# Earlier weight checks and a flag moved ahead of one group; in the chosen experts the shared rows added by VectorE and the inverse roots taken for two tiles together

## The chip, the core and the metric

One core of a Trainium2 chip runs the whole program. The metric is the device time of that core in microseconds; lower is better. PE is TensorE's matmul side and PEld its weight loads, DVE is VectorE, ACT is ScalarE, POOL is GpSimd, SP is SyncE, which here issues most DMAs.

## The reference, cut to what matters

Four residual layers over x of 16 x 512 rows of 128 numbers. The first is attention, the second a gated MLP with ternary weights, the third a mixing layer by Fourier transforms, the fourth a mixture of eight experts of which each row takes one, beside a shared expert:

```python
x = x + _layernorm(attention(_layernorm(x), ...))
x = x + _layernorm(ternary_mlp(_layernorm(x), ...))
x = x + _layernorm(fourier_mix(_layernorm(x), ...))
# the fourth layer, on h = _layernorm(x)
shared_out = swiglu(h, shared_gate, shared_up, shared_down)
logits = h @ gate_w.T
top_id = argmax(logits); score = sigmoid(max(logits))
routed_out = swiglu(h * score, r_gate[top_id], r_up[top_id], r_down[top_id])
x = x + _layernorm(shared_out + routed_out)
```

`swiglu(x, wg, wu, wd)` is `silu(x @ wg.T) * (x @ wu.T) @ wd.T`, with 256 hidden numbers. Everything is fp32.

## The kernel before

**Stages.** The program runs through attention (64 groups: 16 chunks of 512 rows, four groups of heads each), the MLP in pairs of chunks, the mixing and the routing, and last the chosen experts. Each engine has a program of its own, written by hand, and the engines meet at semaphores. An engine works strictly in the order written: whatever waits holds back everything behind it on that engine.

**The flag between attention and MLP.** The MLP's matmuls run on weights cast to another format (`wb`) if no weight was changed by the cast, else on the raw ones. `check_weights(n)` in `att_vector` compares one of NWB = 11 pieces on DVE (L909, `w_diff`, and L912, `rounded`). Attention's groups 64, 65 and 66 (GROUPS + 0, 1, 2) only drain the pipeline, and DVE does the checks at their ends: four, four and three. After them `mlp_vector` sets `ahead_in`, for which ACT waits before it casts the first x (L1186), reduces `rounded` to `any_rounded` (L1274), and waits for PE. PE, in `att_tensor`, has done its groups up to 65 and then waits for `any_rounded` (a matmul that sums it over partitions, L693). Behind that wait stand PE's last P*V products (L608), the transposes of the attention output OT (L618) that ACT copies first (L710), and the first layer of the MLP (L1029). DVE turns PE's sum into `exact_w` (L1276), PE loads it and branches.

**The chosen experts.** The routing has scattered rows of 385 numbers to DRAM, sorted by expert: the scaled input (`0:E`), the shared expert's result (`E:2E`), the residual (`2E:3E`), and the row's number. 72 tiles of 128 such rows are worked through by `tile_steps`: at step i an engine does, in the order of its list, stage s for tile i - lag. The lists (lag, stage) are:

- SP: (0, load) into a ring of RING = 10 slots, `rows7`; the load of tile j waits until `add_residual` of tile j - 10 is done.
- PE: (0, turn_x) L1712, (3, turn_h) L1727, (4, reduce), (1, expand) L1719. `reduce` puts the shared rows into PSUM by a matmul with the identity (L1733) and adds the expert's last layer (L1736).
- ACT: (7, normalise) L1875, (0, copy_xT7), (3, copy_hT), (1, silus) L1861.
- DVE: (8, add_residual) L2103, (2, gate) L2077, (6, bias7) L2097, (5, stats) with bn_stats L2086, bn_aggr L2089 and the add of epsilon L2091, (0, take_idx) L2070.
- POOL: (5, inverse_std), `rs` = `ve` to the power -1/2, L1911, and (8, scatter_out), an indirect DMA of the finished rows, L1917.

In the names that the rows print, `big` is `rows7`, `csum` is the output tile `o7`, and the digits of `st7`, `mv7`, `ve7`, `rs7`, `nb7`, `g7`, `h7` are left out.

Of the kernel before, what the change touches and what calls it, by code (L numbers as in the profile page):

```python
# [5 lines left out]
P = 128  # L6
# [8 lines left out]
ds = bass.ds  # L15
# [43 lines left out]
def block_kernel(nc, io, out):  # L59
# [26 lines left out]
    with top:  # L86
# [3 lines left out]
        def sb(name, shape, dt=F32, ctx=top):  # L90
            return ctx.enter_context(nc.sbuf_tensor(name, shape, dt))
# [757 lines left out]
        def att_vector(dve):  # L849
# [64 lines left out]
            def step(b, i, g, has):  # L914
# [38 lines left out]
                if isinstance(g, int):  # L953
                    for n in range(NWB):
                        if g == GROUPS + n // 4:
                            check_weights(n)
            return run_groups(dve, step, 3)
# [313 lines left out]
        def mlp_vector(dve, group):  # L1271
            dve.memset(ahead_in[:], 0.0).then_inc(ahead_set, 1)
            dve.wait_ge(w_checked, 2 * NWB)
            dve.tensor_reduce(any_rounded[:], rounded[:], AX_X, ALU.max).then_inc(exact_steps, 1)  # L1274
# [137 lines left out]
        RING = 10  # L1412
# [3 lines left out]
        rows7 = big[:, 0:RING * ROW].rearrange("p (k r) -> p k r", k=RING)  # L1416
# [70 lines left out]
        mv7 = sb("mv7", [P, 4, 2], F32, p5)  # L1487
        ve7 = sb("ve7", [P, 4], F32, p5)
# [5 lines left out]
        row_in = [sem(f"row_in{k}") for k in range(RING)]  # L1494
# [33 lines left out]
        with nc.Block() as block:  # L1528
            @block.sync
            def _(sp):  # L1530
# [33 lines left out]
                sp.wait_ge(kv_done, NCH)  # L1564
                sp.wait_ge(out5_done, NCH)
# [9 lines left out]
            def _(pe):  # L1575
# [132 lines left out]
                def turn_x(j):  # L1708
                    pe.wait_ge(row_in[j % RING], j // RING * 16 + 16)
                    if j:  # L1710
                        pe.wait_ge(xT7_set, j)
                    pe.transpose(PS[:, X_BANK, 0:P], rows7[:, j % RING, 0:E], idf[:]).then_inc(turned7, 1)  # L1712
# [17 lines left out]
                def reduce(j):  # L1730
                    if j >= 4:
                        pe.wait_ge(n7_set, j - 3)
                    pe.matmul(PS[:, Y_BANKS[j % 4], 0:E], idf[:], rows7[:, j % RING, E:2 * E], start=True, stop=False)  # L1733
                    pe.wait_ge(hT7_set, j + 1)
                    for f in range(FB1):
                        mm = pe.matmul(PS[:, Y_BANKS[j % 4], 0:E], hT7[:, j % 2, f, :],  # L1736
                                       wdn[:, ds(experts[j] * (FB1 * E) + f * E, E)], start=False, stop=(f == FB1 - 1))
                    mm.then_inc(y7_done, 1)
# [11 lines left out]
            def _(act):  # L1750
# [119 lines left out]
                def normalise(j):  # L1870
                    s = j % 4
                    act.wait_ge(nb7_set, j + 1)
                    if j >= HELD:
                        act.wait_ge(o7_out[j % HELD], j // HELD * 16)
                    act.activation(o7[:, j % HELD, :], PS[:, Y_BANKS[s], 0:E], ACT.Identity,  # L1875
                                   bias=nb7[:, s:s + 1], scale=rs7[:, s:s + 1]).then_inc(n7_set, 1)
                tile_steps([(7, normalise), (0, copy_xT7), (3, copy_hT), (1, silus)])

            @block.gpsimd
            def _(pool):  # L1880
# [25 lines left out]
                def inverse_std(j):  # L1906
                    s = j % 4
                    pool.wait_ge(ve7_set, j + 1)
                    if j >= 4:
                        pool.wait_ge(n7_set, j - 3)  # L1910
                    pool.tensor_tensor(rs7[:, s:s + 1], ve7[:, s:s + 1], neg_half[:, 0:1],  # L1911
                                       ALU.pow).then_inc(rs7_set, 1)
# [7 lines left out]
                tile_steps([(5, inverse_std), (8, scatter_out)])  # L1920
# [4 lines left out]
            def _(dve):  # L1925
# [142 lines left out]
                def take_idx(j):  # L2068
                    dve.wait_ge(row_in[j % RING], j // RING * 16 + 16)
                    dve.tensor_copy(idx7[:, j:j + 1], rows7[:, j % RING, 3 * E:3 * E + 1]).then_inc(idx7_set, 1)  # L2070
# [9 lines left out]
                def stats(j):  # L2080
                    dve.wait_ge(y7_done, j + 1)
                    if j >= 2:
                        dve.wait_ge(st7_set, 2 * j - 2)
                    if j >= 4:
                        dve.wait_ge(n7_set, j - 3)
                    dve.bn_stats(st7[:, j % 2, :], PS[:, Y_BANKS[j % 4], 0:E]).then_inc(st7_set, 1)  # L2086
                    dve.wait_ge(st7_set, 2 * j + 1)
                    settled(dve)
                    dve.bn_aggr(mv7[:, j % 4, :], st7[:, j % 2, :]).then_inc(st7_set, 1)  # L2089
                    dve.wait_ge(st7_set, 2 * j + 2)  # L2090
                    dve.tensor_scalar(ve7[:, j % 4:j % 4 + 1], mv7[:, j % 4, 1:2], EPS, None,  # L2091
                                      ALU.add).then_inc(ve7_set, 1)

                def bias7(j):
                    s = j % 4
                    dve.wait_ge(rs7_set, j + 1)
                    dve.scalar_tensor_tensor(nb7[:, s:s + 1], mv7[:, s, 0:1], -1.0, rs7[:, s:s + 1],  # L2097
                                             ALU.mult, ALU.mult).then_inc(nb7_set, 1)
# [6 lines left out]
                tile_steps([(8, add_residual), (2, gate), (6, bias7), (5, stats), (0, take_idx)])  # L2105
# [76 lines left out]
```

## Time and profile before

| | |
|---|---|
| median of 3 runs | 1690.49 us (1684.03 to 1691.08) |
| the profiled execution | 1691.9 us, its span 1690.1 us |
| PE busy, PEld | 1541.2 us (91%), 843.8 us |
| DVE, ACT, POOL busy | 1285.4 (76%), 1166.5 (69%), 716.7 us (42%) |
| mean granted TensorE clock | 0.960 |

The span runs from the first to the last instruction. Busy shares are means over stages with different limits, so the two places that the change touches have to be read from their own stretches. The page's slices show them: PE's digit falls to 7 and the granted clock to 8 tenths in the 21st of the 40 slices, where attention ends, and the last four slices hold the chosen experts, where POOL's digit is the highest of the whole page (4, 8, 8, 7).

### The profile page before, as it was taken

Reading aid. Unit: us, or ns where it says so; the run is one execution under the profiler, and the core shown is the slowest. Engines: PE = TensorE matmul, PEld = TensorE weight load, DVE = VectorE, ACT = ScalarE, POOL = GpSimd, SP = SyncE. Lnnn points to the kernel's source line nnn. Section 1 sums busy time; section 2 is a strip of 40 time slices with the busy share of each in tenths; the row PEclk is TensorE's granted clock in tenths of the full one; section 3 lists DMA queues with packets and bytes.
Section 4 is the critical chain, followed back from the end, with each engine's and each line's share of the span. In section 5 each row is a group of like instructions: output and inputs, shape, how many; then the busy total and the mean of one; then the engine's idle time right before and its main releaser. Section 6 shows DMA issues by size and latency. Waiting matters only on the chain. (4 is left out here: it accounts for less than half of the span.)

```text
span 1690.1 us, 34457 instructions
## 1 busy us (share of the span) xinstructions
PE 1541.2 (91%) x8456; PEld 843.8 (50%) x8456; DVE 1285.4 (76%) x3546; ACT 1166.5 (69%) x2450; POOL 716.7 (42%) x1011
## 2 busy tenths in 40 slices
PE   4999999999999999999979999999999978867995
PEld 2333333333333333333347777777745655544764
DVE  4899999999999999989876777777668863313664
ACT  1488888888888888878867777777635544553663
POOL 2224334344343344422353434333344442554887
PEclk7699999999999999989989999999999988997998
DMA  4232333223223232242000000000020001434552
GB/s 122 57 89 78 90 94 88 82 76 92 85 82 100 71 92 84 76 141 55 22 7 7 1 1 0 0 0 0 20 86 1 1 1 38 159 117 124 143 137 66
DMA packets 83649, 109.24 MB, mean 65 GB/s; under 512 B 15947, under 2 KB 48977, under 8 KB 83552
## 3 DMA queue, kind: packets, MB, share of 16 engines
q1 hardware_dynamic: 77152, 91.28, 19.0%
q0 software_dynamic: 6400, 16.82, 2.8%
q8 instruction: 42, 0.69, 0.2%
q14 instruction: 55, 0.45, 0.1%
HBM read 63.24 MB, written 40.08 MB: 61 GB/s over the span
## 5 line engine op out<-in xcount | busy, mean ns | idle before, releaser
L853 DVE TENSOR_REDUCE bmax<-PS 128x8 f32<-128x512 f32 x1024 | 651.2, 682 | 62.9 <-PE PS L587 60.5
L704 ACT ACTIVATE EX<-PS 128x512 f32<-128x512 f32 x1024 | 564.3, 604 | 105.9 <-PE PS L598 96.5
L587 PE MATMUL PS<-KR,QR 33*128 33x512 f32 x1024 | 410.1, 470 | 36.5 <-DVE bmax L853 23.7
L598 PE MATMUL PS<-QR,KR 64*128 64x512 f32 x1024 | 397.9, 461 | 1.8 <-ACT EX L704 1.5
L587 PEld LDWEIGHTS PS<-KR,QR 33*128 33x128 f32 x1024 | 167.1, 190 | 351.1 <-DVE bmax L853 296.5
L608 PE MATMUL PS<-EX,VS 128*9 128x512 f32 x2048 | 271.6, 602 | 0.0
L598 PEld LDWEIGHTS PS<-QR,KR 64*128 64x128 f32 x1024 | 162.4, 186 | 11.9 <-ACT EX L704 10.2
L1029 PE MATMUL PS<-pA,wb 128*128 128x512 f32 x640 | 151.7, 393 | 0.0
L789 POOL TENSOR_TENSOR m_diff<-m_prev,m_all 128x16 f32<-128x16 f32 x64 | 14.2, 222 | 314.3 <-DVE m_all L865 314.3
L1204 ACT ACTIVATE gelud<-PS,scales 128x512 f32<-128x512 f32 x128 | 88.2, 689 | 64.0 <-PE PS L1029 63.9
L1029 PEld LDWEIGHTS PS<-pA,wb 128*128 128x128 f32 x640 | 118.4, 188 | 23.8
L1029 PE MATMUL PS<-pB,wb 128*128 128x512 f32 x512 | 117.7, 389 | 0.0
L1147 POOL CAST pA<-gated 128x512 fp32r<-128x512 f32 x64 | 57.1, 891 | 130.4 <-DVE gated L1283 129.8
L1029 PEld LDWEIGHTS PS<-pB,wb 128*128 128x128 f32 x512 | 96.0, 188 | 19.9
L1889 POOL DMA_INDIRECT row_scr<-row,idx x64 | 61.7, 964 | 59.2 <-ACT row L1833 21.7
L1917 POOL DMA_INDIRECT out<-csum,idx x72 | 74.4, 1033 | 16.5 <-issue 13.0
L1029 PE MATMUL PS<-pX,wb 128*128 128x512 f32 x256 | 69.0, 409 | 8.7 <-DVE gated L1283 7.5
L1719 PE MATMUL PS<-wgu,xT 128*128 x144 | 76.0, 610 | 0.0
L2019 DVE TENSOR_TENSOR qq<-PS,kA 128x512 f32<-128x512 f32 x32 | 21.6, 689 | 68.5 <-ACT kA L1816 48.2
L608 PEld LDWEIGHTS PS<-EX,VS 128*9 128x9 f32 x2048 | 30.4, 88 | 80.7 <-ACT EX L704 41.3
L1283 DVE SCALAR_TENSOR_TENSOR gated<-PS,scales,sil 128x512 f32<-128x512 f32 x64 | 47.5, 748 | 29.1 <-ACT sil L1178 18.5
L1178 ACT ACTIVATE sil<-PS,scales 128x512 f32<-128x512 f32 x64 | 43.8, 687 | 34.2 <-PE PS L1029 34.1
(231 smaller groups left out, 2806.5 us busy)
## 6 DMA issues: line engine op xcount, KB each, us to landing
QR<-q_scr SPq DMA_DIRECT2D x256, 64.0 KB, 2.5
KR<-k_scr SPq DMA_DIRECT2D x256, 64.0 KB, 2.4
big<-row_scr SPq DMA_DIRECT2D x72, 192.5 KB, 2.3
k_scr<-partsB SPq DMA_DIRECT2D x42, 256.0 KB, 2.9
q_scr<-partsB SPq DMA_DIRECT2D x28, 256.0 KB, 2.9
X<-in_L_attn_x SPq DMA_DIRECT2D x16, 256.0 KB, 2.9
X<-x SPq DMA_DIRECT2D x16, 256.0 KB, 2.5
xB<-in_L_attn_x SPq DMA_DIRECT2D x14, 256.0 KB, 3.3
```

The costliest lines, as they stand in the source:

```text
L587: pe.matmul(PS[:, bank_of(i, n), :], QR[rows, i, h // 2, t * P:(t + 1) * P], KR[rows, i, h // 2, :], start=True, stop=True).then_inc(tile_ ...
L598: pe.matmul(PS[:, RING3 + bank_of(j, n), :], KR[rows, j, h // 2, kt * P:(kt + 1) * P], QR[rows, j, h // 2, :], start=True, stop=True).then ...
L608: mm = pe.matmul(PS[32 * h:32 * h + HD + 1, 6, :], VS[:, j, kt, h, :], EX[:, kt % 2 * HG + head_T(h), :], start=(kt == 0), stop=(kt == NT ...
L704: act.activation(EX[:, n % (2 * HG), :], PS[:, RING3 + bank_of(j, n), :], ACT.Exp, scale=SCALE).then_inc(ex_set, 1)
L853: dve.tensor_reduce(bmax[:, i % 2, n, :], PS[:, bank_of(i, n), :].rearrange("p (b k) -> p b k", k=BLK), AX_X, ALU.max).then_inc(tile_max, 1)
L1029: mm = pe.matmul(bank, lhs, rhs, start=(n == 0), stop=(n == len(todo) - 1))
L1147: pool.tensor_copy(pA[:, s, f, 0, :], gated[:, n % HR, :]).then_inc(hi0_set, 1)
L1204: act.activation(gelud[:, f, :], PS[:, f, :], ACT.Gelu, scale=scales[:, 2 + layer, f:f + 1]).then_inc(gelu_set, 1)
L1283: dve.scalar_tensor_tensor(gated[:, n % HR, :], PS[:, 2 * (n % 2) + 1, :], scales[:, 1, n % FB:n % FB + 1], sil[:, n % 2, :], ALU.mult, AL ...
L1719: pe.matmul(PS[:, GU_BANKS[s], :], xT7[:, s, :], wgu[:, ds(experts[j] * (2 * F1), 2 * F1)], start=True, stop=True).then_inc(gu7_done, 1)
L1889: pool.indirect_dma_start(out=row_scr, out_offset=bass.IndirectOffsetOnAxis(idx[:, c * NT + t:c * NT + t + 1], 0), in_=row[:, s, t, :], in ...
L1917: pool.indirect_dma_start(out=out_rows, out_offset=bass.IndirectOffsetOnAxis(idx7[:, j:j + 1], 0), in_=o7[:, j % HELD, :], in_offset=None, ...
```

## The change

Seam between attention and MLP: seven checks stand at the end of group 64 and four at the end of group 65, none at 66; behind the four stand the setting of `ahead_in` and the reduction to `any_rounded`. Chosen experts: PE no longer adds the shared rows; DVE adds them as it reads the result from PSUM into a new tile `y7`, and the statistics (now `moments`, a stage of its own at the list's end) and ACT's `normalise` read `y7` from SBUF. Epsilon, inverse root and bias are done once for two tiles, at the odd one. `normalise` goes from lag 7 to 8, `add_residual` and `scatter_out` from 8 to 9. The ring of loaded rows moves into X and has 12 slots, and SP drops two waits ahead of the first load.

```diff
@@ att_vector, step
                     for n in range(NWB):
-                        if g == GROUPS + n // 4:
+                        if g == GROUPS + (n > NT + 2):
                             check_weights(n)
+                    if g == GROUPS + 1:
+                        dve.memset(ahead_in[:], 0.0).then_inc(ahead_set, 1)
+                        dve.wait_ge(w_checked, 2 * NWB)
+                        dve.tensor_reduce(any_rounded[:], rounded[:], AX_X, ALU.max).then_inc(exact_steps, 1)
@@ mlp_vector
-            dve.memset(ahead_in[:], 0.0).then_inc(ahead_set, 1)
-            dve.wait_ge(w_checked, 2 * NWB)
-            dve.tensor_reduce(any_rounded[:], rounded[:], AX_X, ALU.max).then_inc(exact_steps, 1)
             dve.wait_ge(exact_steps, 2)
@@ buffers, SP
-        RING = 10
+        RING = 12
-        rows7 = big[:, 0:RING * ROW].rearrange("p (k r) -> p k r", k=RING)
+        rows7 = X[:, 0:RING * ROW].rearrange("p (k r) -> p k r", k=RING)
+        y7 = sb("y7", [P, 4, E], F32, p5)
-                sp.wait_ge(kv_done, NCH)
-                sp.wait_ge(out5_done, NCH)
@@ PE, reduce
-                        pe.wait_ge(n7_set, j - 3)
-                    pe.matmul(PS[:, Y_BANKS[j % 4], 0:E], idf[:], rows7[:, j % RING, E:2 * E], start=True, stop=False)
+                        pe.wait_ge(st7_set, 3 * j - 11)
@@ ACT, normalise
-                    act.wait_ge(nb7_set, j + 1)
+                    act.wait_ge(nb7_set, j // 2 + 1)
-                    act.activation(o7[:, j % HELD, :], PS[:, Y_BANKS[s], 0:E], ACT.Identity,
+                    act.activation(o7[:, j % HELD, :], y7[:, s, :], ACT.Identity,
-                tile_steps([(7, normalise), (0, copy_xT7), (3, copy_hT), (1, silus)])
+                tile_steps([(8, normalise), (0, copy_xT7), (3, copy_hT), (1, silus)])
@@ POOL
                 def inverse_std(j):
-                    s = j % 4
-                    pool.wait_ge(ve7_set, j + 1)
+                    if j % 2 == 0:
+                        return
+                    k, s = j // 2, (j - 1) % 4
+                    pool.wait_ge(ve7_set, k + 1)
                     if j >= 4:
                         pool.wait_ge(n7_set, j - 3)
-                    pool.tensor_tensor(rs7[:, s:s + 1], ve7[:, s:s + 1], neg_half[:, 0:1],
+                    pool.tensor_tensor(rs7[:, s:s + 2], ve7[:, s:s + 2], neg_half[:, 0:2],
                                        ALU.pow).then_inc(rs7_set, 1)
-                tile_steps([(5, inverse_std), (8, scatter_out)])
+                tile_steps([(5, inverse_std), (9, scatter_out)])
@@ DVE
                 def stats(j):
                     dve.wait_ge(y7_done, j + 1)
-                    if j >= 2:
-                        dve.wait_ge(st7_set, 2 * j - 2)
                     if j >= 4:
                         dve.wait_ge(n7_set, j - 3)
-                    dve.bn_stats(st7[:, j % 2, :], PS[:, Y_BANKS[j % 4], 0:E]).then_inc(st7_set, 1)
-                    dve.wait_ge(st7_set, 2 * j + 1)
+                    dve.tensor_tensor(y7[:, j % 4, :], PS[:, Y_BANKS[j % 4], 0:E], rows7[:, j % RING, E:2 * E],
+                                      ALU.add).then_inc(st7_set, 1)
+
+                def moments(j):
+                    dve.wait_ge(st7_set, 3 * j + 1)
+                    dve.bn_stats(st7[:, j % 2, :], y7[:, j % 4, :]).then_inc(st7_set, 1)
+                    dve.wait_ge(st7_set, 3 * j + 2)
                     settled(dve)
                     dve.bn_aggr(mv7[:, j % 4, :], st7[:, j % 2, :]).then_inc(st7_set, 1)
-                    dve.wait_ge(st7_set, 2 * j + 2)
-                    dve.tensor_scalar(ve7[:, j % 4:j % 4 + 1], mv7[:, j % 4, 1:2], EPS, None,
-                                      ALU.add).then_inc(ve7_set, 1)
+                    if j % 2 == 1:
+                        s = (j - 1) % 4
+                        dve.wait_ge(st7_set, 3 * j + 3)
+                        dve.tensor_scalar(ve7[:, s:s + 2], mv7[:, s:s + 2, 1], EPS, None,
+                                          ALU.add).then_inc(ve7_set, 1)
...
-                tile_steps([(8, add_residual), (2, gate), (6, bias7), (5, stats), (0, take_idx)])
+                tile_steps([(9, add_residual), (5, stats), (2, gate), (6, bias7), (0, take_idx), (5, moments)])
```

On DVE, at the ends of groups 65 and 66, before (the last check of group 65, then the statistics of the next chunk's residual `x`, then the first of group 66's three checks):

```order
L912 TENSOR_TENSOR rounded<-rounded,w_diff 128x512
L123 BN_STATS ln_st<-x 128x6 x4
L873 SCALAR_TENSOR_TENSOR den<-corr,OTT 128x16
L152 BN_AGGR ln_mv<-ln_st 128x2 x4
L878 RECIPROCAL rden<-den 128x16
L886 TENSOR_TENSOR AOs<-OTT,rden 128x4x32
L909 TENSOR_TENSOR w_diff<-w_raw,wb 128x512
L912 TENSOR_TENSOR rounded<-rounded,w_diff 128x512
```

and, two such pairs of rows further on:

```order
L912 TENSOR_TENSOR rounded<-rounded,w_diff 128x512
L1272 MEMSET ahead_in 128x2
L1274 TENSOR_REDUCE any_rounded<-rounded 128x1
L1276 TENSOR_SCALAR exact_w<-PS 1x1
L1288 TENSOR_TENSOR pX<-XT,pX 128x512 x2
```

and now, from the last check of group 65:

```order
L912 TENSOR_TENSOR rounded<-rounded,w_diff 128x512
L958 MEMSET ahead_in 128x2
L960 TENSOR_REDUCE any_rounded<-rounded 128x1
L123 BN_STATS ln_st<-x 128x6 x4
L873 SCALAR_TENSOR_TENSOR den<-corr,OTT 128x16
L152 BN_AGGR ln_mv<-ln_st 128x2 x4
L878 RECIPROCAL rden<-den 128x16
L886 TENSOR_TENSOR AOs<-OTT,rden 128x4x32
L1277 TENSOR_SCALAR exact_w<-PS 1x1
L1289 TENSOR_TENSOR pX<-XT,pX 128x512 x2
```

The flag has moved ahead of that chunk's statistics; three checks have moved to the end of group 64, ahead of everything DVE does in group 65.

On DVE, one step of the chosen experts before, in the steady part:

```order
L2103 TENSOR_TENSOR csum<-csum,big 128x128
L2077 TENSOR_TENSOR h<-PS,g 128x256
L2097 SCALAR_TENSOR_TENSOR nb<-mv,rs 128x1
L2086 BN_STATS st<-PS 128x6
L2089 BN_AGGR mv<-st 128x2
L2091 TENSOR_SCALAR ve<-mv 128x1
L2070 CAST idx<-big 128x1
```

and two steps now, an even one and an odd one (`X` is now also the name of the ring, `y` is `y7`):

```order
L2112 TENSOR_TENSOR csum<-csum,X 128x128
L2086 TENSOR_TENSOR y<-PS,X 128x128
L2079 TENSOR_TENSOR h<-PS,g 128x256
L2072 CAST idx<-X 128x1
L2091 BN_STATS st<-y 128x6
L2094 BN_AGGR mv<-st 128x2
L2098 TENSOR_SCALAR ve<-mv 128x2
L2112 TENSOR_TENSOR csum<-csum,X 128x128
L2086 TENSOR_TENSOR y<-PS,X 128x128
L2079 TENSOR_TENSOR h<-PS,g 128x256
L2106 SCALAR_TENSOR_TENSOR nb<-mv,rs 128x2
L2072 CAST idx<-X 128x1
```

The add of the shared rows is new; `ve` and `nb` come in every second step; the statistics follow the gate and the index copy, where they stood between them.

On POOL, the chosen experts before and, in the second fence, now:

```order
L1917 DMA out<-csum,idx 8192x128
L1911 TENSOR_TENSOR rs<-ve,neg_half 128x1
L1917 DMA out<-csum,idx 8192x128
L1911 TENSOR_TENSOR rs<-ve,neg_half 128x1
L1917 DMA out<-csum,idx 8192x128
```

```order
L1913 TENSOR_TENSOR rs<-ve,neg_half 128x2
L1919 DMA out<-csum,idx 8192x128 x2
L1913 TENSOR_TENSOR rs<-ve,neg_half 128x2
L1919 DMA out<-csum,idx 8192x128 x2
L1913 TENSOR_TENSOR rs<-ve,neg_half 128x2
```

One root on two columns stands ahead of two scatters, which now follow each other directly.

## Rows read from the trace of the kernel before

**Rows 1.** Chain of waits, 1530 to 1690 us, shares by engine and line

```profile
by line: PE PS L1719 38.4%; PE PS L1736 18.4%; PE PS L1727 9.4%; PE PS L1733 9.2%; PE PS L1712 5.2%; issue 4.6%; POOL out L1917 3.2%; POOL rs L1911 1.7%; DMA big<-row_scr 1.5%; DVE csum L2103 0.8%; DVE st L2086 0.6%; DVE mv L2089 0.4%; ACT 
```

**Rows 2.** Busy time in a stretch of the expert stage

```profile
core 0: us, PE busy (x) PEld busy (x) DVE busy (x) ACT busy (x) POOL busy (x), PEclk, DMA share, GB/s
...
1580.00:1600.00 20.00, 20.00 (x122) 14.44 (x121) 13.94 (x77) 12.50 (x44) 17.38 (x23) 1.00 0.51 143
```

**Rows 3.** Order of time, one step of the expert stage: start, duration, engine, line

```profile
1602.59 0.28 DVE L2103 TENSOR_TENSOR csum<-csum,big 128x128 f32<-128x128 f32 x1
...
1602.71 0.59 POOL L1911 TENSOR_TENSOR rs<-ve,neg_half 128x1 f32<-128x1 f32 x1
...
1602.97 0.39 PE L1733 MATMUL PS<-big,idf 128*128 128x128 f32 x2
...
1603.19 0.61 PE L1736 MATMUL PS<-wdn,hT 128*128 x4
1603.26 0.42 DVE L2077 TENSOR_TENSOR h<-PS,g 128x256 f32<-128x256 f32 x1 [0.39 <-ACT g L1861]
...
1603.51 1.03 POOL L1917 DMA_INDIRECT out<-csum,idx  x1 [0.21 <-issue]
...
1603.66 0.29 DVE L2086 BATCH_NORM_STATS2 st<-PS 128x6 f32<-128x128 f32 x1
1604.10 0.18 DVE L2089 BATCH_NORM_AGGREGATE mv<-st 128x2 f32<-128x6 f32 x1
...
1604.32 0.15 DVE L2091 TENSOR_SCALAR ve<-mv 128x1 f32<-128x1 f32 x1
...
1604.45 0.28 DVE L2103 TENSOR_TENSOR csum<-csum,big 128x128 f32<-128x128 f32 x1
...
1604.57 0.59 POOL L1911 TENSOR_TENSOR rs<-ve,neg_half 128x1 f32<-128x1 f32 x1
```

**Rows 4.** Order of time around the flag, 834 to 865 us

```profile
834.10 0.71 DVE L909 TENSOR_TENSOR w_diff<-w_raw,wb 128x512 f32<-128x512 f32 x1
...
838.68 0.69 DVE L909 TENSOR_TENSOR w_diff<-w_raw,wb 128x512 f32<-128x512 f32 x1
...
843.91 0.69 DVE L897 TENSOR_TENSOR y<-PS,bias 128x512 f32<-128x512 f32 x1 [3.80 <-PE PS L623]
...
846.24 0.69 DVE L909 TENSOR_TENSOR w_diff<-w_raw,wb 128x512 f32<-128x512 f32 x1
...
852.09 0.82 DVE L912 TENSOR_TENSOR rounded<-rounded,w_diff 128x512 f32<-128x512 f32 x1
...
860.82 0.69 DVE L1274 TENSOR_REDUCE any_rounded<-rounded 128x1 f32<-128x512 f32 x1
860.84 1.14 ACT L1186 CAST pX<-XT 128x512 fp32r<-128x512 f32 x2 [5.97 <-DVE ahead_in L1272]
...
861.65 0.16 PE L693 MATMUL PS<-any_rounded 128*1 128x1 f32 x1 [7.90 <-DVE any_rounded L1274]
...
863.66 0.58 ACT L710 COPY OT<-PS 128x512 f32<-128x512 f32 x1 [0.16 <-PE PS L608]
864.29 1.11 PE L618 MATMUL PS<-idf,OT 128*128 128x128 f32 x4 [0.73 <-ACT OT L710]
```

**Rows 5.** Busy time and granted clock (PEclk), columns as in Rows 2

```profile
865.40:871.43 6.03, 6.03 (x19) 4.73 (x19) 3.52 (x8) 3.08 (x5) 1.51 (x2) 0.61 0.00 0
917.45:922.06 4.61, 4.14 (x18) 2.80 (x16) 3.17 (x5) 2.80 (x5) 2.23 (x3) 1.00 0.00 0
```

**Rows 6.** Groups of POOL by shape, the inverse roots

```profile
L1911 POOL TENSOR_TENSOR rs<-ve,neg_half 128x1 f32<-128x1 f32 x72 | 42.0, 583 | 22.0 <-DVE ve L2091 19.9
...
L166 POOL TENSOR_TENSOR ln_rs<-ln_ve,neg_half 128x4 f32<-128x4 f32 x18 | 18.2, 1010 | 95.7 <-DVE ln_ve L132 95.7
```

**Rows 7.** Order of time, POOL at the end of the kernel

```profile
1679.96 0.97 POOL L1917 DMA_INDIRECT out<-csum,idx  x1 [0.30 <-issue]
```

**Rows 8.** DMA issues of the page, the row loads: count, KB, us to landing

```profile
big<-row_scr SPq DMA_DIRECT2D x72, 192.5 KB, 2.3
```

More of the change, by code:

```diff
@@ L1493, in block_kernel @@
         hs = qq
-        row_in = [sem(f"row_in{k}") for k in range(RING)]
+        row_in = [sem(f"row_in{k}") for k in range(RING - 2)] + mrow_in
+        ROWS_FROM = [0] * (RING - 2) + [GROUPS // 2 * 32] * 2
         score_set = sem("score_set")
@@ L1708, in turn_x @@
                 def turn_x(j):
-                    pe.wait_ge(row_in[j % RING], j // RING * 16 + 16)
+                    pe.wait_ge(row_in[j % RING], ROWS_FROM[j % RING] + j // RING * 16 + 16)
                     if j:
@@ L1736, in reduce @@
                         mm = pe.matmul(PS[:, Y_BANKS[j % 4], 0:E], hT7[:, j % 2, f, :],
-                                       wdn[:, ds(experts[j] * (FB1 * E) + f * E, E)], start=False, stop=(f == FB1 - 1))
+                                       wdn[:, ds(experts[j] * (FB1 * E) + f * E, E)], start=(f == 0), stop=(f == FB1 - 1))
                     mm.then_inc(y7_done, 1)
@@ L2068, in take_idx @@
                 def take_idx(j):
-                    dve.wait_ge(row_in[j % RING], j // RING * 16 + 16)
+                    dve.wait_ge(row_in[j % RING], ROWS_FROM[j % RING] + j // RING * 16 + 16)
                     dve.tensor_copy(idx7[:, j:j + 1], rows7[:, j % RING, 3 * E:3 * E + 1]).then_inc(idx7_set, 1)
@@ L2081, in stats @@
                     dve.wait_ge(y7_done, j + 1)
-                    if j >= 2:
-                        dve.wait_ge(st7_set, 2 * j - 2)
                     if j >= 4:
                         dve.wait_ge(n7_set, j - 3)
-                    dve.bn_stats(st7[:, j % 2, :], PS[:, Y_BANKS[j % 4], 0:E]).then_inc(st7_set, 1)
-                    dve.wait_ge(st7_set, 2 * j + 1)
+                    dve.tensor_tensor(y7[:, j % 4, :], PS[:, Y_BANKS[j % 4], 0:E], rows7[:, j % RING, E:2 * E],
[4 more added lines that the diff above has]
+                    dve.wait_ge(st7_set, 3 * j + 2)
                     settled(dve)
                     dve.bn_aggr(mv7[:, j % 4, :], st7[:, j % 2, :]).then_inc(st7_set, 1)
-                    dve.wait_ge(st7_set, 2 * j + 2)
-                    dve.tensor_scalar(ve7[:, j % 4:j % 4 + 1], mv7[:, j % 4, 1:2], EPS, None,
-                                      ALU.add).then_inc(ve7_set, 1)
-                def bias7(j):
-                    s = j % 4
-                    dve.wait_ge(rs7_set, j + 1)
-                    dve.scalar_tensor_tensor(nb7[:, s:s + 1], mv7[:, s, 0:1], -1.0, rs7[:, s:s + 1],
+                    if j % 2 == 1:
[3 more added lines that the diff above has]
+                                          ALU.add).then_inc(ve7_set, 1)
+                def bias7(j):
+                    if j % 2 == 0:
+                        return
+                    s = (j - 1) % 4
+                    dve.wait_ge(rs7_set, j // 2 + 1)
+                    dve.scalar_tensor_tensor(nb7[:, s:s + 2], mv7[:, s:s + 2, 0], -1.0, rs7[:, s:s + 2],
                                              ALU.mult, ALU.mult).then_inc(nb7_set, 1)
```

## The prediction

> **What bounds the kernel now.** The page's slices name two places, and I read each in its own stretch.
>
> *Chosen experts.* The chain of waits over the last 160 us runs over PE's five lines of the stage, 77.0% together [rows 1], and in a stretch of 20 us PE is busy for all 20.00 [rows 2]: PE sets the step. The step is 1.86 us, from one residual add on DVE (1602.59) to the next (1604.45) [rows 3]. Of it, the product with the identity that brings in the shared rows takes 1603.19 - 1602.97 = 0.22 us. The reader should then look at who comes second, since that one takes over. It is POOL. Its root starts at 1602.71 and lasts 0.59, the scatter starts at 1603.51 and lasts 1.03, the next root starts at 1604.57: 0.21 us between root and scatter, 0.03 between scatter and root, and nothing left of 1.86 [rows 3]. By busy time alone POOL shows 17.38 of 20 and looks as if it had room [rows 2]. DVE waits 0.39 us of each step for ACT, and ACT is busy for 12.50 of 20.
>
> *Seam.* In order of time around the flag, PE's flag product at 861.65 has waited 7.90 us for `any_rounded`, and ACT's cast of x has waited 5.97 us for `ahead_in`, so since 854.87 [rows 4]. DVE was busy with checks all that time. PE then runs at a low clock: the first layer's 16 products take 6.03 us at a mean of 0.61 of full speed, and the same work of a later chunk 4.61 us at full clock, waits included [rows 5].
>
> **The flag.** A check takes (838.68 - 834.10) / 3 = 1.53 us where POOL is idle [rows 4]. Seven of them end at 834.10 + 10.7 = 844.8, where DVE began group 65's bias add at 843.91, so everything of group 65 on DVE comes 0.9 us later. PE does not wait for that add before it waits for ACT's exponentials. The four checks there ended at 852.09 + 0.82 = 852.91, now at 853.8; with 0.06 and 0.69 behind them the flag is there at about 854.6, where it was there at 861.5. PE's flag product thus comes 6.9 us earlier.
>
> That is not the gain, because ACT is late next. It is free at 854.87, casts x (1.14), loads a table and gets to the copy of OT. It did so 863.66 - 0.16 = 863.50 after starting at 860.84; shifted by 5.97 that is 857.53. PE's transposes follow at 864.29 - 863.66 + 857.53 = 858.16. They took 1.11 at the low clock; at full clock I take 0.5 to 0.6, and the first layer starts at 858.7 instead of 865.40: 6.7 us. DVE, meanwhile, has four statistics, four aggregates, some small instructions and one half of x to do behind the flag; with 0.29 and 0.18 for one of the first two [rows 3] and 0.69 for 512 numbers [rows 4] I estimate 3 us from 854.6, which is inside 858.7. Queued behind DVE's first seven checks there is nothing that PE needs.
>
> Then the clock. Idle until the flag is now 0.9 us and not 7.90, and about 2 us more go by before the OT copy. If the clock stays up, the first layer costs 4.61 and not 6.03 (1.4 us more gained). If it falls, the transposes and the layer keep their old cost and the seam gives 6.1. Against this I set 0 to 1.0 us: POOL gets the residual 0.9 us later and normalises it in front of its first cast of `gated`, while that cast is wanted 7 us earlier. Seam: 6.7 + 1.4 - 0.5 = **7.6 us**, bounds 5.1 and 8.1.
>
> The Trainium skill says in "SBUF — State Buffer", section "Who interferes with whom", that a VectorE instruction with two SBUF inputs contends with a GpSimd instruction that reads SBUF. Here such a check piece takes 0.69 us at 838.68 and 0.82 at 852.09, beside POOL's normalising [rows 4]: the trace agrees. By it three checks moved to where POOL is idle save some 0.4 us. The same section lets an instruction with one SBUF input, as the new add of a PSUM bank and shared rows, pass POOL without contention, and no run here shows that yet.
>
> **The experts' step on each engine.**
>
> PE: 1.86 - 0.22 = 1.64 us. `reduce` loses one wait and gets an earlier one; nothing else of PE moves.
>
> DVE: a start follows 0.08 us before its forerunner's end (`ve`, 0.15 long, and one instruction like it fit between 1604.32 and 1604.45). So `csum` takes 0.20, `h` 0.34, `st` 0.44 to the start of `mv`, `mv` 0.22 to that of `ve`, and `ve`, `nb` and the index 0.065 each [rows 3]. The new add of 128 numbers, half PSUM, is not in the trace. It lies between `csum` (128 numbers, SBUF) and `h` (256, half PSUM): 0.20 to 0.34. I take 0.20, since 128 more numbers are what `h` has over it. An even step is then 0.20 + 0.20 + 0.34 + 0.065 + 0.44 + 0.22 + 0.065 = 1.53, an odd one less: under PE's 1.64, at the dear end just over it (1.67).
>
> POOL, for two tiles: root, 0.21, scatter, gap, scatter, 0.03. The scatters' gap is not in the steady trace; at the end of the kernel, where they follow each other, it is 0.30 [rows 6]. The root on two columns is not in the trace either: one column takes 0.583, four take 1.010 [rows 7], so a straight line gives 0.73; bounds 0.58 and 1.01. Sum: 0.73 + 0.21 + 1.03 + 0.30 + 1.03 + 0.03 = 3.33, **1.66 us a tile**, just above PE. Bounds 3.18 (1.59, and PE's 1.64 rules) and 3.61 (1.80). So of the 0.22 that PE gives up, 0.20 are realised and POOL becomes the bound.
>
> The Trainium skill, in "GPSIMD Engine Reference", section "Elementwise — side-by-side cycle accounting", gives GpSimd about 2.6 cycles an element for two inputs, by which a second column would cost next to nothing. The rows of the root say 0.14 us a column, so the measurement decides; by the page the sum would be rival A below.
>
> The round trip between the two: after `rs`, DVE does `nb`, index, `st`, `mv`, `csum`, add, `h`, index, `st`, `mv`, `ve`, some 2.3 us to the next `ve`. POOL needs 0.21 + 1.03 + 0.30 + 1.03 + 0.03 = 2.60 to be free again, so `ve` is there first, by 0.3 us.
>
> ACT reads `y7` from SBUF instead of PSUM and has 7.5 of 20 us free. SP's dropped waits were for events long past, behind the scatter to DRAM. A row load lands after 2.3 us [rows 8]; it was issued two steps ahead, with 12 slots and one lag more it is three, 5 us. These cost nothing, behind PE and POOL; without that cover a late load would cost about 1 us once.
>
> **Sum.** Steps 4 to 71 run at the steady pace, 67 x (1.86 - 1.66) = 13.4 us. At the end POOL has, from step 71 on, four roots and eleven scatters instead of seven and ten: 3 x 3.33 + 0.73 + 0.21 + 5 x 1.03 + 4 x 0.30 = 17.3 against 7 x 1.86 + 3 x 1.27 = 16.8, so 0.5 back. Experts 12.9, seam 7.6: **20.5 us**. The profiled execution took 1691.9, which gives 1671.4; the median is 1.4 lower, so **1670.0**.
>
> **Rivals.**
>
> A, PE stays the bound (chance 0.20). The second column is nearly free, POOL needs 1.59 and PE's 1.64 rules: 67 x 0.22 = 14.7, the end as before; with the seam 22.3, **1668**. For it: only the two ends 0.583 and 1.010 are measured.
>
> B, the root on two columns costs as one on four, or the added DVE work delays each root by as much (0.13): 1.80 us a tile, 67 x 0.06 = 4.0, 1.6 back at the end, seam 7.6, gain 10.0: **1680.5**.
>
> C, the experts give nothing (0.06): a 192.5 KB load every 1.66 us beside the scatters does not keep up and the step stays 1.86. DMA's share is 0.51 now and would be 0.57, which speaks against it. Only the seam is left: **1683**.
>
> D, slower (0.03). DVE's way from `rs` to the next `ve` misses POOL and the two run in turn. It decides only from 0.3 us beyond my 2.3; slower than before needs a pair over 3.72 + 0.23 = 3.95, so a way of 3.2, 0.9 more than the rows give. At 4.4 a pair the loss is 67 x 0.34 = 23, less the seam: **1706**. The dear add alone gives two times 0.14.
>
> My forecast, POOL at 1.66, has 0.58; its own range is 1666 to 1675.
>
> **How the numbers follow.** The forecast and A reach from 1665 to 1675, with B to 1681; what is left out is C, D and some of the scatter of the runs (1684.03 to 1691.08 before). Range 1661 to 1680. A change under 0.5% (8.5 us) is about what a measurement of this kernel cannot tell from none: C and a corner of B fall there, 0.07; slower 0.03; faster 0.90.
>
> **What would show it.** In the profile after: `any_rounded` near 854.6 and PE's wait for it under 1.5 us; the first layer starting near 858.7, its clock at 1.00 or at 0.50; root 128x2 at 0.73; a pair of scatters with 0.30 between; a PE step of 1.66 with short idle pieces, where now there are none; waits of `nb` for `rs`. Wrong it would be if DVE's idle time before `h` is gone and POOL waits for `ve`, if the step is not between 1.63 and 1.70, or if the first layer starts later than 860.

## The result, and the profile after

| | us |
|---|---|
| before, median of 4 runs beside it (range) | 1690.53 (1684.03 to 1691.08) |
| after, median of 4 runs (range) | 1669.33 (1666.57 to 1674.57) |
| ratio, 95% interval | 0.9885, 0.9869 to 0.9902 |
| profiled execution, span before and after | 1690.1 and 1667.5 |

The kernel became faster, by 21.2 us; 20.5 were forecast. To see where they come from I cut both spans at the same instructions: DVE's last `m_all` of attention (833.29 before, 832.39 after), PE's first product with `pA` (878.52 and 871.45), POOL's first scatter into `row_scr` (1412.9 and 1406.1), its last (1526.4 and 1516.9), and the end.

| stretch | before, us | after, us | difference |
|---|---|---|---|
| attention, up to `m_all` | 833.3 | 832.4 | 0.9 |
| seam, to the first product with `pA` | 45.2 | 39.1 | 6.2 |
| MLP and routing, to the first row scatter | 534.4 | 534.6 | -0.2 |
| scatters of rows, first to last | 113.4 | 110.8 | 2.6 |
| experts, from the last row scatter to the end | 163.7 | 150.6 | 13.1 |

The stretches add up to 22.6 us between these two executions. The change touches only the seam and the experts: 19.3 us. The other 3.3 are scatter between two executions: in the second group of kernels below, the scatters of rows took 94.8 to 98.4 us on one chip with the same instructions. The chain of the changed kernel over the same last stretch as [rows 1]:

```profile
by line: issue 47.4%; POOL out L1919 34.1%; POOL rs L1913 3.4%; PE PS L1720 2.5%; PE PS L1736 1.3%; POOLq L1919 0.8%; POOLq L106 0.7%; PE PS L1728 0.6%; ACTq L1531 0.6%; DVE h L2079 0.6%; DVE csum L2112 0.5%; DVE st L2091 0.5%; DVE mv L2094
```

PE's five lines held 80.6% of it before (the sum of the row in [rows 1]; the prediction says 77.0%); now POOL's scatter leads, with "issue", time for which the profile shows no wait. PE's busy share doesn't tell the two kernels apart: it is full in the same 20 us as in [rows 2].

```profile
1580.00:1600.00 20.00, 20.00 (x110) 13.29 (x109) 16.33 (x85) 14.96 (x50) 16.51 (x19) 1.00 0.55 160
```

One pair of tiles in order of time, POOL and DVE (answers to [rows 3]):

```profile
1641.50 0.98 POOL L1919 DMA_INDIRECT out<-csum,idx  x1 [0.30 <-issue]
1642.11 0.37 DVE L2098 TENSOR_SCALAR ve<-mv 128x2 f32<-128x2 f32 x1
...
1642.56 0.72 POOL L1913 TENSOR_TENSOR rs<-ve,neg_half 128x2 f32<-128x2 f32 x1
...
1643.32 0.16 DVE L2106 SCALAR_TENSOR_TENSOR nb<-mv,rs 128x2 f32<-128x2 f32 x1 [0.30 <-POOL rs L1913]
...
1643.48 1.04 POOL L1919 DMA_INDIRECT out<-csum,idx  x1 [0.20 <-issue]
...
1643.99 0.29 DVE L2112 TENSOR_TENSOR csum<-csum,X 128x128 f32<-128x128 f32 x1
...
1644.83 0.98 POOL L1919 DMA_INDIRECT out<-csum,idx  x1 [0.30 <-issue]
...
1645.63 0.17 DVE L2098 TENSOR_SCALAR ve<-mv 128x2 f32<-128x2 f32 x1
1645.71 0.29 DVE L2112 TENSOR_TENSOR csum<-csum,X 128x128 f32<-128x128 f32 x1
1645.89 0.72 POOL L1913 TENSOR_TENSOR rs<-ve,neg_half 128x2 f32<-128x2 f32 x1
1645.92 0.28 DVE L2086 TENSOR_TENSOR y<-PS,X 128x128 f32<-128x128 f32 x1
```

Root to root takes 3.33 us for two tiles, and POOL stops only for 0.20, 0.30 and 0.08. DVE waits for POOL now, 0.30 us before `nb`. One pair later `ve` comes earlier:

```profile
1648.15 0.98 POOL L1919 DMA_INDIRECT out<-csum,idx  x1 [0.30 <-issue]
...
1648.43 0.17 DVE L2098 TENSOR_SCALAR ve<-mv 128x2 f32<-128x2 f32 x1
...
1649.14 0.74 POOL L1913 TENSOR_TENSOR rs<-ve,neg_half 128x2 f32<-128x2 f32 x1
```

Here the root stands 0.99 us behind the start of the scatter (1649.14 - 1648.15), above 1.06 (1642.56 - 1641.50), and this pair of tiles takes 3.25 us (1649.14 - 1645.89). So POOL's own work for two tiles is about 3.25, and the usual 3.33 holds 0.07 more, in which the root follows a `ve` that lands late. In 24 of the 36 cases `ve` starts about 0.6 us into the second scatter, lasts 0.35 to 0.37 us instead of 0.17, and ends with the scatter.

The groups by shape (answer to the root's row; the prediction's text names the roots' prices as rows 7 and the gap of 0.30 as rows 6, which stand the other way round):

```profile
L1913 POOL TENSOR_TENSOR rs<-ve,neg_half 128x2 f32<-128x2 f32 x36 | 26.0, 723 | 23.1 <-DVE ve L2098 20.7 <-issue 0.2
```

Around the flag, in order of time (answers to [rows 4]):

```profile
843.69 0.68 DVE L897 TENSOR_TENSOR y<-PS,bias 128x512 f32<-128x512 f32 x1
...
852.77 0.69 DVE L960 TENSOR_REDUCE any_rounded<-rounded 128x1 f32<-128x512 f32 x1
853.61 0.19 PE L693 MATMUL PS<-any_rounded 128*1 128x1 f32 x2 [0.77 <-DVE any_rounded L960]
853.84 1.14 ACT L1190 CAST pX<-XT 128x512 fp32r<-128x512 f32 x2
...
855.00 1.28 ACT L1187 ACT_TABLE_LOAD   x1
...
856.40 0.57 ACT L710 COPY OT<-PS 128x512 f32<-128x512 f32 x1
857.02 1.12 PE L618 MATMUL PS<-idf,OT 128*128 128x128 f32 x4 [1.97 <-ACT OT L710]
858.01 6.33 PE L1033 MATMUL PS<-pX,wb 128*128 128x512 f32 x16
```

PE waits 0.77 us for the flag, and 1.97 for the copy of OT, which stands on ACT behind the cast and the table. The clock over the same stretch (PE's busy time, then the granted clock; [rows 5] has that of before):

```profile
855.00:856.00 1.00, 0.05 (x4) 1.00 0.68 262
856.00:857.00 1.00, 0.00 (x0) 0.69 0.00 0
857.00:863.00 6.00, 5.98 (x16) 0.50 0.00 0
863.00:864.00 1.00, 1.00 (x6) 0.90 0.00 0
```

It fell to 0.50, the lower of the two levels (1.2 of 2.4 GHz), while PE stood idle in front of OT, and came back after some six busy microseconds. The forecast had named this case, but its sum has the other one.

### The profile page after: what moved, and what is told of

It reads as the page before. It is cut to its first block, busy times and chain, and to the rows that moved or that the text cites. A ratio compares the mean times of both kernels' runs of the same rounds, so it can differ in the third digit from the quotient of the medians.

```text
span 1667.5 us, 34164 instructions
## 1 busy us (share of the span) xinstructions
PE 1527.0 (92%) x8312; PEld 831.1 (50%) x8312; DVE 1288.8 (77%) x3546; ACT 1171.0 (70%) x2450; POOL 700.1 (42%) x975
## 4 chain that ended last, share of the span: by engine, by line
PE 63%; DVE 14%; issue 9%; ACT 5%; POOL 4%; SPq 1%; another core or an unknown queue 1%; DMA 1%; DVEq 0%; POOLq 0%; ACTq 0%
PE PS L1033 18%; PE PS L587 14%; PE PS L608 12%; DVE bmax L853 6%; PE PS L598 4%; PE PS L618 3%; POOL out L1919 3%; PE PS L623 2%; PE PS L1676 1%; PE PS L1688 1%; PE PS L1677 1%; ACT y L1780 1%; PE PS L647 1%; PE PS L649 1%
## 5 line engine op out<-in xcount | busy, mean ns | idle before, releaser
L587 PE MATMUL PS<-KR,QR 33*128 33x512 f32 x1024 | 409.1, 469 | 38.3 <-DVE bmax L853 24.3
```

The source lines that it names most:

```text
L587: pe.matmul(PS[:, bank_of(i, n), :], QR[rows, i, h // 2, t * P:(t + 1) * P], KR[rows, i, h // 2, :], start=True, stop=True).then_inc(tile_ ...
```

## The experiments

Three groups of four, each group on one chip with runs of the kernel before beside it. The kernel before took 1673.71, 1671.79 and 1689.14 us there, so kernels of different groups are compared by ratio, or by the same stretch inside the traces.

**Seam alone** (the DVE part of the diff up to the flag, on the kernel before).

> The kernel before with the checks and the flag moved, experts untouched. My theory (both parts independent, the seam gives what ACT lets it give): the MLP's first layer starts some 7 us earlier after attention's last reduction than before, its clock at 0.50 as in the profile after, and 6.1 us less in all, so about 1684.4 against 1690.5; the expert step stays 1.86. Rival (the seam's gain is given back later, and all of the 21 us come from the experts): within 1 us of before.

1667.76 us, ratio 0.9961 (0.9949 to 0.9973). The seam took 38.3 us against 45.0 in the run below, the experts 164.7: the step of before. The rival, a gain given back later, would have been within 1 us of before.

**Experts alone** (all of the diff from `RING` on).

> The changed kernel with checks and flag back where they were. My theory: 13 us less than before, about 1677.5, step 1.66, PE's wait for the flag 7.9 us again. Rival (part of the 13 us came from the routing stage, which ran 2.5 us shorter in the profile after, as an effect of the change): the routing stage's length, from the first to the last scatter of rows, is the same as in the profile after, and not spread by chance.

1661.41 us, ratio 0.9932 (0.9914 to 0.9949). Seam 45.0 us, experts 150.5. Against each other these two runs give 6.7 us for the seam and 14.1 for the experts, and each part gives about what it gives in the whole change. In every kernel of this group the scatters of rows take 14 to 17 us less than in the first two profiles (97 against 113.4 and 110.8 us), on which see the last section.

**The product back on PE**, everything else as changed: does POOL alone set the step?

```diff
+                    pe.matmul(PS[:, Y_BANKS[j % 4], 0:E], idf[:], rows7[:, j % RING, E:2 * E], start=True, stop=False)
...
-                    dve.tensor_tensor(y7[:, j % 4, :], PS[:, Y_BANKS[j % 4], 0:E], rows7[:, j % RING, E:2 * E],
-                                      ALU.add).then_inc(st7_set, 1)
+                    dve.tensor_copy(y7[:, j % 4, :], PS[:, Y_BANKS[j % 4], 0:E]).then_inc(st7_set, 1)
```

> The changed kernel, but PE adds the shared rows again by its product with the identity and DVE only copies the sum to y7; roots stay in pairs. My theory (PE's own time is the floor of the step): step 1.86 again, PE busy without gaps, POOL waiting; experts as before the change, some 13 us over the changed kernel, about 1682. Rival (it was POOL's pairing that shortened the step): step 1.66 to 1.70, and within 3 us of the changed kernel.

1665.13 us, ratio 0.9958 (0.9937 to 0.9979), as the seam alone. POOL in order of time:

```profile
1599.93 1.04 POOL L1920 DMA_INDIRECT out<-csum,idx  x1 [0.20 <-issue]
...
1601.27 0.98 POOL L1920 DMA_INDIRECT out<-csum,idx  x1 [0.30 <-issue]
1602.73 0.72 POOL L1914 TENSOR_TENSOR rs<-ve,neg_half 128x2 f32<-128x2 f32 x1 [0.47 <-DVE ve L2098]
1603.64 1.04 POOL L1920 DMA_INDIRECT out<-csum,idx  x1 [0.20 <-issue]
```

The pair takes 3.71 us (1603.64 - 1599.93), 1.86 a tile: POOL now has room and waits for `ve`, since PE sets the pace. The loss is the stage's 12.1 us (162.7 against 150.6), near the 13 expected.

**Roots one by one** (epsilon and bias too), the product still off PE.

```diff
...
-                    pool.tensor_tensor(rs7[:, s:s + 2], ve7[:, s:s + 2], neg_half[:, 0:2],
+                    pool.tensor_tensor(rs7[:, s:s + 1], ve7[:, s:s + 1], neg_half[:, 0:1],
...
```

> The changed kernel, but epsilon, root and bias tile by tile as before (root 128x1), with the lags of the changed kernel; PE without its identity product. My theory (POOL's root, scatter and gaps are 1.83 to 1.86 a tile): step 1.83 to 1.86, waits of DVE for rs, PE with gaps of 0.2 us a step; some 12 us over the changed kernel, about 1681.5. Rival (PE's product was the whole gain): step 1.66 and no more than 2 us over the changed kernel.

1664.83 us, ratio 0.9942 (0.9922 to 0.9961).

```profile
1601.58 0.59 POOL L1911 TENSOR_TENSOR rs<-ve,neg_half 128x1 f32<-128x1 f32 x1
1602.35 1.03 POOL L1917 DMA_INDIRECT out<-csum,idx  x1 [0.18 <-issue]
1603.41 0.58 POOL L1911 TENSOR_TENSOR rs<-ve,neg_half 128x1 f32<-128x1 f32 x1
```

Step 1.83 us, and POOL has no gap but its usual ones (0.18 and 0.03). The 0.2 us gaps of PE that I expected don't show: PE is busy for 20.00 and 19.72 us in two stretches of 20, so here too its busy share doesn't tell who sets the step. So each half of the experts' part, alone, leaves the stage at 162.7 and 162.3 us; together it is 150.6. The two engines stood at 1.86 and 1.83, and both had to go down.

**The changed kernel again**, and **the power replaced by a product** (leaves out the inverse root of the experts' norm).

> The changed kernel, unaltered, beside the edits of it on this chip. From the first four runs, in which the step of the experts is 1.86 us with the product on PE, 1.83 with single roots and 1.66 with both parts of the change, and the seam in two halves of the change is worth about 6 us: ratio to the kernel before near 0.988, seam 6.1 us earlier, clock of the first layer at 0.50.

> The changed kernel with the power on POOL replaced by a product of the same two columns: it leaves out the inverse root of the experts' norm. Theory (POOL is the bound at 1.66 us a tile, PE's floor is 1.64 just under it): POOL's pair falls by what the root gets cheaper, some 0.4 us and more, POOL gets waits, PE rules, and the step falls only from 1.66 to 1.64: 1 to 2 us in all, with PE busy for all of a stretch again. Rival: something else than POOL or PE sets 1.66, and the step doesn't change; or PE's floor is lower than 1.64, and the gain is over 3 us.

Again: 1652.28 us, ratio 0.9881 (0.9859 to 0.9903). Cheap root: 1647.59, ratio 0.9846 (0.9825 to 0.9867). A stretch of the cheap root's stage, and behind it the group of its roots:

```profile
1580.00:1600.00 20.00, 20.00 (x111) 13.53 (x111) 17.06 (x88) 14.76 (x51) 13.04 (x19) 1.00 0.58 163
```

```profile
L1913 POOL TENSOR_TENSOR rs<-ve,neg_half 128x2 f32<-128x2 f32 x36 | 7.0, 195 | 25.3 <-DVE ve L2098 24.3
```

The root falls from 0.72 to 0.20 us, POOL's busy time in 20 us from 16.5 to 13.04, and most pairs take 3.27 us instead of 3.33: 1.635 a tile. POOL now has room (14 waits for `ve` in 60 us), so this pace is another engine's, and it fits the 1.64 computed for PE. The stage is 4.8 us shorter and not the 1 to 2 expected. Against the changed kernel on the same chip, the first 27 pairs give 1.1 us, the last eight 2.3, where POOL works off what has piled up, and the stretches before the first root and behind the last one 0.8 and 0.6.

**The add done twice** on DVE, the first into a scratch tile.

> The changed kernel with the add of the shared rows done twice on DVE (the first into a scratch tile). One more start costs 0.21 us (csum to y, y to h in the trace of the changed kernel), so DVE's even step goes from 1.53 to 1.74 and its odd one from 1.46 to 1.67 or so. Theory (DVE is a third engine close behind POOL at 1.66 and PE at 1.64, with about 0.13 us to spare): DVE becomes the bound and the step is 1.71 to 1.76, 3 to 7 us slower than the changed kernel in all. Rival: DVE's waits (0.3 us each second step for the root, and for ACT) don't shrink because they are part of the round trip with POOL, the pair grows by the full 0.4 us and more, and the loss is 12 us and over.

1672.78 us, ratio 0.9905 (0.9868 to 0.9942); the experts took 151.2 us against 151.0 and 151.1 in the two kernels with the unaltered expert part on that chip. In order of time:

```profile
1561.24 0.18 DVE L2096 BATCH_NORM_AGGREGATE mv<-st 128x2 f32<-128x6 f32 x1 [0.50 <-issue]
1561.35 0.29 DVE L2114 TENSOR_TENSOR csum<-csum,X 128x128 f32<-128x128 f32 x1
1561.56 0.28 DVE L2087 TENSOR_TENSOR y<-PS,X 128x128 f32<-128x128 f32 x1
1561.76 0.28 DVE L2088 TENSOR_TENSOR y<-PS,X 128x128 f32<-128x128 f32 x1
1561.95 0.41 DVE L2080 TENSOR_TENSOR h<-PS,g 128x256 f32<-128x256 f32 x1
...
1562.78 0.18 DVE L2096 BATCH_NORM_AGGREGATE mv<-st 128x2 f32<-128x6 f32 x1
1562.99 0.17 DVE L2100 TENSOR_SCALAR ve<-mv 128x2 f32<-128x2 f32 x1
...
1563.28 0.28 DVE L2087 TENSOR_TENSOR y<-PS,X 128x128 f32<-128x128 f32 x1
```

A start of the add costs the 0.20 us of the forecast, but neither theory held: the usual pair stays at 3.33 us. The equal length of the stage hides a small loss: from the first root to the last it is 119.2 us, against 117.5 and 117.6 in those two kernels, since six pairs take 3.5 to 3.7; before the first root this execution is 1.5 us shorter than theirs. This step, the one with `ve`, is 1.72 long (1563.28 - 1561.56). In the other `csum` follows `mv` after 0.11 us (1561.35 - 1561.24), where `ve` stands 0.21 behind it (1562.99 - 1562.78), so it needs some 0.06 less than my 1.67: 1.72 and 1.61 are just the pair's 3.33. `nb` no longer waits for the root over 80 us of the stage, since DVE comes to it later, and `ve`, which starts 0.2 us later in its scatter (0.81 us into it), is no longer held and ends at the same point.

**Ten slots instead of twelve.**

```diff
-        RING = 12
+        RING = 10
```

> The changed kernel with 10 slots for rows instead of 12; residuals still nine tiles behind. Theory (the two slots are what hides the loads): a slot is free one step ahead of its tile instead of three, the load takes 2.3 us, and the step grows from 1.66 to what the loop of residual, load and turning needs, 2.3 to 2.8 us: 45 to 80 us slower than the changed kernel, with PE waiting for the rows each step. Rival: the load is hidden anyway, and the step stays at 1.66.

1702.79 us, ratio 1.0074 (1.0053 to 1.0094): slower than the kernel before. PE's wait for rows over 100 us of the stage (sum, times, longest), which the changed kernel doesn't have in that list:

```profile
PEld PS L1713 <- DMA X<-row_scr: 42.8, 40, 2.1
```

The mechanism is that of the theory, the size smaller: the stage took 182.1 us, 31 more and not 45 to 80, a step of about 2.1 and not 2.3 to 2.8. PE's weight load waits for rows 40 times, 1.07 us on average; for part of that time PE's products still run, whose own waits for rows are 12.5 us. The two slots are a needed part of the change.

**Extra products on PE** in the 1.97 us before OT.

```diff
+                        for n in range(7):
+                            pe.matmul(PS[:, 1, :], QR[0:HALF, 3, 0, 0:P], KR[0:HALF, 3, 0, :], start=True, stop=True)
```

> The changed kernel with seven extra 64-row products of 128 x 512 on PE (0.25 us each, into a bank that nobody reads) in the 1.97 us in which PE waits for ACT's copy of OT. Theory: the clock falls because PE is idle there; with the extra products it stays at 1.00, the transposes of OT take 0.6 instead of 1.12 us and the first layer 4.6 instead of 6.0, so everything behind the seam is 1.4 to 1.9 us earlier than in the changed kernel, the size of the clock term of the prediction. Rival: the first layer is held by its operands (DVE's low parts, the silu) and not by the clock, and the gain is under 0.5 us; or the clock falls all the same, because of the 0.77 us idle before the flag, and nothing is gained.

```profile
855.00:857.00 2.00, 1.56 (x8) 1.00 0.00 0
857.00:860.00 3.00, 2.46 (x10) 1.00 0.00 0
860.00:863.00 3.00, 2.23 (x13) 1.00 0.00 0
```

The clock stays at 1.00, OT's transposes take 0.65 us, and the seam 37.4 us. The changed seam took 38.3 to 39.1 in eight traces (mean 38.7), according to how long the clock was down: 38.3 to 38.6 in the four where it was low for 3.4 us, 38.9 to 39.1 in the four where it was low for 6.8. So products in the idle time before OT keep it up, and the fallen clock costs 0.9 to 1.7 us, 1.3 on average.

**The table behind the copy of OT**, and **the table and four extra products**.

> The changed kernel with ACT's load of the silu table (1.28 us and 0.20 for the activation that calls for it) behind the copy of OT instead of ahead of it. Theory (the seam is limited by ACT once the flag is early): OT is copied from 855.1 us on, PE's wait for it falls from 1.97 to about 0.6 us, the first layer starts when DVE's low parts are there, near 857.2 instead of 858.0; 0.8 us, and 1.4 to 1.9 more if the clock then stays up. Rival: PE only waits for the low parts instead of for OT, for as long as before, and the clock falls as before: 0.8 us or less.

> The changed kernel with the silu table behind the copy of OT, and two extra 64-row products of 0.25 us on PE ahead of the turning of OT and two behind it. Alone, the later table made the first layer start 1.05 us earlier at a clock that fell all the same (first pA product 1.35 us earlier than in the unaltered one), and extra products alone kept the clock at 1.00 (1.2 us earlier). Theory: together they add up, clock at 1.00 throughout and the first pA product 2.2 to 2.7 us earlier than in the unaltered kernel, which is near what the prediction wanted of the seam. Rival: with OT early, DVE's low parts and POOL's first cast of gated hold the layer, and it is no more than 1.5 us; the time of the whole kernel can't tell this apart from no change.

Table later: OT is turned 2.15 us behind the flag instead of 3.42, PE waits 0.71 us for it instead of 1.97, and the clock falls all the same, for 3.4 us; seam 37.2 us. So the drop doesn't need a wait of 2 us. With extra products the clock stays at 1.00 and AOs is turned 9.42 us behind the flag (11.45 in the changed kernel on its second chip), yet the seam is 37.2 again: the two gains don't add up. Why, in order of time:

```profile
858.34 3.29 POOL L808 TENSOR_SCALAR xn<-x,ln_mv,ln_rs 128x128 f32<-128x128 f32 x4 [0.21 <-POOL ln_rs L160]
...
861.58 1.18 POOL L1158 CAST pA<-gated 128x512 fp32r<-128x512 f32 x2
...
862.23 1.07 DVE L1295 TENSOR_TENSOR pA<-gated,pA 128x512 fp32r<-128x512 f32 x1 [1.89 <-POOL pA L1158]
...
864.10 4.95 PE L1040 MATMUL PS<-pX,wb 128*128 128x512 f32 x16 [0.37 <-DVE gated L1290]
```

POOL normalises ahead of its first cast of `gated`, DVE waits 1.89 us for that cast, and PE's next layer for DVE. In whole kernels the three seam edits gave 0.9891 (0.9860 to 0.9922), 0.9878 (0.9857 to 0.9900) and 0.9873 (0.9835 to 0.9911): no difference from the unaltered one that these runs can tell. The 1.2 us of the extra products are still there at MLP's end, whose last product starts 356.6 us behind the flag against 357.8. In the next stage PE waits again, and around 1217 us its clock is at 0.68 with the extra products and at 1.00 in the changed kernel on the same chip; from MLP's end to the first scatter of a row it is 195.4 us against 193.0 (all traces lie between), so that scatter comes 1.3 us later with the extra products and not 1.2 earlier.

**Checks seven and four, the flag at its old place.**

```diff
-                    if g == GROUPS + 1:
-                        dve.memset(ahead_in[:], 0.0).then_inc(ahead_set, 1)
-                        dve.wait_ge(w_checked, 2 * NWB)
-                        dve.tensor_reduce(any_rounded[:], rounded[:], AX_X, ALU.max).then_inc(exact_steps, 1)
...
```

> The changed kernel with the checks seven and four, but the flag where it was, behind all of DVE's work of the last attention groups. Theory (two steps: the regrouping brings the flag forward to where ACT's end of the exponentials is nearly the limit, moving the flag itself past DVE's statistics and small work brings the rest): the flag is reduced near 855.9 instead of 852.8 in the profile of the changed kernel, OT is turned some 2 us later than there, and the seam is worth about 4 of its 6.1 to 6.5 us. Rival: the checks are late whatever the grouping, and without the move nothing is gained (6 us lost); or ACT is the limit in both cases and nothing is lost.

1672.49 us, ratio 0.9901 (0.9865 to 0.9936).

```profile
854.58 0.16 PE L693 MATMUL PS<-any_rounded 128*1 128x1 f32 x1 [3.81 <-DVE any_rounded L1274]
```

The flag is 24.3 us behind `m_all`, 3.05 later than with the move, 4.1 earlier than before; the seam is 40.8 us. Of the 6.4 us that the seam gives on average (45.1 to 38.7), the regrouping gives 4.3 and the move 2.1, by this one trace. The ratio can't be told from that of the changed kernel.

No version that keeps the root beats the changed kernel by more than its runs scatter.

## Why the prediction was right, and where it was off

*The sum.* 20.5 forecast, 19.3 in the parts that the change touches, 21.2 between the medians. The forecast case, a step of 1.66 with POOL in front, is the one that happened. That the medians meet within 0.7 us is partly luck: the seam gave 1.4 less than forecast, and scatter in stretches that the change doesn't touch is of the same size.

*The flag.* Forecast 6.9 us earlier on PE; 861.65 - 853.61 = 8.04, of which 0.9 came from attention: 7.1. DVE's 3.80 us idle before the bias add [rows 4] are gone, filled with checks, as laid out.

*ACT next.* Forecast: PE is held by OT's copy, first layer 6.7 us earlier, waiting for the flag under 1.5. It waits 0.77, then 1.97 for OT, and the layer starts at 858.01, 7.4 earlier and 6.5 without attention's 0.9. Shown by the later table, which brings OT forward 1.3 us.

*The clock.* The term that failed is the +1.4 for a clock that stays up. It fell, and the transposes took 1.12 us, not 0.5 to 0.6. The prediction's sentence for this case, "the transposes and the layer keep their old cost and the seam gives 6.1", is what the trace shows: 6.2 (6.4 as the mean of all traces). With the clock kept up by extra products the seam gives 45.1 - 37.4 = 7.7 against the 7.6 of the sum. Both cases and their price were right, the choice between them was not: the prediction names both waits, 0.9 us and about 2 more, and then puts the full 1.4 into the sum without a row that shows the clock staying up over them. The later table shows that even 0.77 and 0.71 us, with 1 us of products between, don't keep it up.

*POOL's cast*, 0 to 1.0 us. The sum has 0.5 for it. In the changed kernel it is hidden behind the slow layer, and it is plain as soon as the rest is faster (1.89 us of DVE's wait).

*The experts.* Forecast 12.9, measured 13.1 (14.1 on a second chip). Root 0.73, measured 0.72; gap 0.30, measured 0.30; pair 3.33, measured 3.33; new add 0.20, measured 0.20 to 0.21; DVE from `rs` to the next `ve` 2.3, measured 1645.63 - 1643.32 = 2.31; PE's floor 1.64, measured 1.635 with the cheap root.

That the pair came out at 3.33 is luck in one term. The second scatter takes 0.98 and not 1.03, so POOL's own work is about 3.25 a pair, 1.63 a tile and no more than PE's 1.64. What lifts the pair above PE's pace is the 0.07 us before the root. The prediction's margin, "`ve` is there first, by 0.3 us", is the step that doesn't hold: its 2.3 us are right, but they end at the start of `ve`, and `ve` then lasts up to 0.37 and ends 0.09 before the root. That is shown by the order of time alone; no run moves `ve` ahead by itself. Of the signs in the prediction, the idle pieces of PE didn't come either: PE is busy for 20.00 of 20 us.

*A slip.* The shares of PE's five lines in [rows 1] add up to 80.6%, not to 77.0%; nothing else rests on it.

*The rivals.* A (PE stays the bound) needed a nearly free second column; at 0.14 us it isn't, and the cheap root shows A's pace once the root is cheap. B fell with the root at 0.72. C fell: the loads keep up with 12 slots, though not with 10. D (the two run in turn) didn't happen: with 0.2 us more on DVE's way from `rs` to `ve` the usual pair is still 3.33, as the double add shows. But little of D's margin is left.

*The Trainium skill.* By "GPSIMD Engine Reference", section "Elementwise — side-by-side cycle accounting", a second column would be nearly free. The product of the same shape took 0.20 us and the power 0.72, so most of the power's time is beyond what that section counts for an element. "SBUF — State Buffer", section "Who interferes with whom", lets an add with one SBUF input pass POOL: it took 0.28 us in all 24 steps between 1600 and 1640 us, though it overlaps the root on POOL in one step of two and the scatter in others, so the trace agrees.

## What to carry to other kernels

When two engines stand within a few hundredths of a step of each other, cut both or none: either half of this change alone gave 0.03 us a step at most, both gave 0.20. Before counting a shortened wait, list the waits behind it on the same engine: here the wait for the flag fell from 7.90 to 0.77 us, and PE's clock still fell over what remained. One or two microseconds at a seam are read from the stretch between two fixed instructions; the whole kernel's time could not show them. Compare the end, not the start, of what an engine waits for: `ve` started 0.45 us ahead of the root and ended 0.09 ahead.

## What was not expected of the hardware

The stretch from the first to the last of 64 row scatters took 94.8 to 98.4 us in the eight traces of two chips and 110.8 to 113.4 in the other traces, with the same instructions. That is about the 15 to 19 us between the medians of the kernel before (1671.8 and 1673.7, against 1689.1 and 1690.5). In each of the long ones ACT waits four times for 3.0 to 5.2 us before it fills the row buffer (`row`), for something that the profile doesn't name; in the short ones it waits there for earlier scatters, mostly 1.5 to 3.0 us and once 4.2. Why a chip should differ in this stays open.

Indirect scatters that follow each other on POOL leave 0.30 us between them, and 0.18 to 0.21 in most cases behind a root that is a power, whatever the kernel.

In the changed kernel `ve`, a small instruction of DVE, ends with POOL's second scatter when it starts 0.6 to 0.8 us into it: it is 0.37 us long at 0.61, 0.22 at 0.75 and 0.17 at 0.80, but also 0.17 when it starts at 0.4 or earlier. The next instruction on DVE starts 0.08 us behind it as always, so only its end is late. The one-column `ve` keeps its 0.15 us beside the scatters of the kernel before. What holds the wider one stays open.
